# Attention with an adapter: one stacked fp32r product for the adapter's values, three orders moved, the causal mask in bf16

## The chip, the cores and the metric

The kernel runs on one core of a Trainium2 chip. The metric is the device time of one execution in microseconds; the time before is 2753.98 us, the median of three runs. Shorter is better.

## The reference, cut to what matters

One block of a transformer: adaLN, attention with an adapter, projection, then a mixture of experts. T = 2048 tokens, C = 1024, 32 heads of 32 columns, 10 adapter rows. The part that the change touches is this:

```python
scores = jnp.einsum('bhqd,bhkd->bhqk', q, k) / jnp.sqrt(jnp.asarray(hd, x.dtype))
scores = jnp.where(causal, scores, jnp.asarray(-jnp.inf, x.dtype))
attn = jax.nn.softmax(scores, axis=-1)
y = jnp.einsum('bhqk,bhkd->bhqd', attn, v)
...
ascores = jnp.einsum('bhqd,xhkd->bhqk', q, ak) / jnp.sqrt(jnp.asarray(C, x.dtype))
ascores = gating[0] * jax.nn.softmax(ascores.astype(jnp.float32), axis=-1).astype(q.dtype)
y = y + jnp.einsum('bhqk,xhkd->bhqd', ascores, av)
```

Everything else (the layernorms, q, k, v, the projection and the experts) is the same before and after.

## The kernel before, in words

Three stages follow one another: `front` (layernorm, modulation, q, k and v, the adapter's probabilities `a_prob` and values `av`), `attention`, and `tail` (projection, router, experts). The diff is in `attention`.

Attention takes four heads at a time (HG = 4, a group; there are G = 8). A unit is one group with one chunk of 512 queries (`qc` of 0 to 3); an iteration `i` of the outer loop has two groups, so W = 8 units and 80 steps. A step is one block of 128 keys of a unit, for four heads: for each head `score` makes the scores product (L1112, with a mask product L1116 on the diagonal), and then `look` works off what `order` lists for this slot. Behind the four slots come `multiply` (probabilities times values of two steps before, into `y_acc`, L1132), and in odd steps `add_up` (the softmax sums, into `total`, L1145).

`order` is a list written out ahead of the loop. Its entries are `see` (a scores product with queries and keys exchanged, L1065, from which VectorE takes the row maxima of a later group, L1278 or, masked, L1284), `turn` (the maxima are transposed), `ask` (the adapter's probabilities of a unit are transposed, L1078) and `give` (the adapter's values times these, L1084). `share` deals the entries of a step to its four slots: the first three get one each, the last gets the rest. Every entry writes one of the three banks of `seen`, in turn; TensorE waits before entry n until VectorE has freed entry n - 3. VectorE frees a bank itself: after a `see` with the reduce, after ask with `keep_turned` (a copy to `a_turn`, L1324), after give with `divide` (y_own times the inverse of the sums, L1332, then the adapter's part added, L1335; the bank is freed at L1314). ask stands in step last+6 of its unit's last step, give in step last+8, both in the second slot of an odd step.

ScalarE makes the exponentials (L1248) and takes `y_acc` and `total` out. GpSimd adds the probabilities of two steps for `add_up` (`two`, L1391, in two halves of two heads) and splits y into a high and a low part (L1397, L1399). SP issues the loads: q and k of the next group (L935), v (L1027), a broadcast of the inverses (L979), the stores of y (L985), `a_prob` for the next ask (L994, step last+3) and `a_v` for the next group (L998, behind the store in step last+9 of every fourth unit). In the last iteration `w_proj` is split too, partly by VectorE (L1356).

Ahead of the loop stands the head: 76 `see` products with their reduces, while SP loads the first group and the constants, and GpSimd scales the adapter's values with `gating` (L1368) and sets rows and buffers (L1371, L1373, L1374).

## Time and profile before

| | |
|---|---|
| median of three runs | 2753.98 us (2748.05 to 2754.27) |
| the profiled execution, its own time | 2743.23 us |
| its span | 2741.4 us |
| TensorE busy | 2517.3 us, 92% |
| VectorE busy | 1617.9 us, 59% |
| GpSimd busy | 1280.5 us, 47% |
| ScalarE busy | 1021.2 us, 37% |

PE is TensorE, PEld its weight loads, DVE is VectorE, ACT is ScalarE, POOL is GpSimd, SPq is SP's queue; a row with q after the engine is the engine's sequencer. A row of the timeline has the start in us from the start of the span, the time it took, the engine, the line, what it wrote and read, how many instructions were merged, and in brackets how long the engine had been idle and what ended that. A row of a group has busy time and mean time in ns, then the idle time before. A row of the stretches has the stretch, its length, the busy time of PE, PEld, DVE, ACT and POOL (with the number of instructions), the granted clock of TensorE as a share of full speed, the DMA engines' share and GB/s.

### The profile page before, as it was taken

To read this page: it belongs to the slowest core of one execution; us is meant where nothing else is said; L and a number is where in the kernel's file an instruction comes from. 1 tells how busy PE (TensorE), PEld (TensorE's weight loads), DVE (VectorE), ACT (ScalarE), POOL (GpSimd) and SP (SyncE) were. 2 spreads that over 40 slices of the span, in tenths; PEclk is the share of its full clock that TensorE was granted. 3 is DMA by queue.
4 is the path that set the end of the run, shared out by engine and by line. 5 is a ranking of instruction groups with operands and counts; after the bars stand their busy time and mean duration, and the time that the engine had idled before them with its cause. 6 is when DMAs were issued, how large, how long until landed. Compare 5 with 4: busy or idle time off the path is not lost. (4 is left out here: it accounts for less than half of the span.)

```text
span 2741.4 us, 39398 instructions
## 1 busy us (share of the span) xinstructions
PE 2517.3 (92%) x13399; PEld 1620.9 (59%) x13399; DVE 1617.9 (59%) x3227; ACT 1021.2 (37%) x1829; POOL 1280.5 (47%) x823
## 2 busy tenths in 40 slices
PE   6799999999599999999999999998979975999997
PEld 4667777777444444444444444444368764888885
DVE  5545565410277666767666766778236654767776
ACT  3421111110035555555555555555601111444443
POOL 4452342200436666666666666665723443333332
PEclk9999999999679999999999999999989987999998
DMA  7356555321624141413233141512356754878885
...
DMA packets 223212, 369.10 MB, mean 135 GB/s; under 512 B 43614, under 2 KB 103070, under 8 KB 222926
## 3 DMA queue, kind: packets, MB, share of 16 engines
...
q14 instruction: 67, 0.55, 0.1%
...
## 5 line engine op out<-in xcount | busy, mean ns | idle before, releaser
L1248 ACT ACTIVATE t_prob<-t_scores_psum 128x512 f32<-128x512 f32 (+3 forms) x1280 | 611.6, 537 | 528.7 <-PE t_scores_psum L1116 286.3
L1391 POOL TENSOR_TENSOR t_two<-t_prob 128x1024 f32<-128x1024 f32 (+1 forms) x321 | 687.1, 2161 | 242.7 <-ACT t_prob L1248 138.8
L1065 PE MATMUL t_seen_psum<-t_k_stack,t_q_stack 96*128 96x512 f32 (+3 forms) x1283 | 524.7, 421 | 60.5 <-DMA t_k_stack<-scratch_k_lo 22.6
L1278 DVE TENSOR_REDUCE t_part<-t_seen_psum 128x1 f32<-128x512 f32 x768 | 482.1, 683 | 158.4 <-PE t_seen_psum L1065 149.5
L1112 PE MATMUL t_scores_psum<-t_q_stack,t_k_stack 97*128 97x512 f32 (+3 forms) x1280 | 505.6, 406 | 5.5 <-ACT t_prob L1248 4.3
L1112 PEld LDWEIGHTS t_scores_psum<-t_q_stack,t_k_stack 97*128 97x128 f32 x1280 | 242.1, 190 | 332.0 <-ACT t_prob L1248 179.3
L1284 DVE CUSTOM_DVE_ANT_0 t_seen_psum<-t_seen_psum,t_causal 128x128 f32<-128x128 f32 (+3 forms) x515 | 248.9, 507 | 140.2 <-PE t_seen_psum L1065 128.0
L1065 PEld LDWEIGHTS t_seen_psum<-t_k_stack,t_q_stack 96*128 96x128 f32 x1283 | 257.2, 201 | 121.8 <-DVEq L1314 36.2
L1132 PE MATMUL t_y_acc_psum<-t_prob,t_v 128*32 128x512 f32 (+3 forms) x2560 | 312.8, 562 | 0.0
L1672 PE MATMUL acc_psum<-z_e_hi,z_x_hi 128*128 128x512 f32 x576 | 227.9, 396 | 0.0
L1674 PE MATMUL acc_psum<-z_e_hi,z_x_lo 128*128 128x512 f32 x576 | 224.9, 390 | 0.0
L1673 PE MATMUL acc_psum<-z_e_lo,z_x_hi 128*128 128x512 f32 x576 | 224.4, 390 | 0.0
L696 PE MATMUL f_acc_psum<-hT_hi,f_w_hi 128*128 128x512 f32 x512 | 209.6, 409 | 1.7 <-POOL f_w_lo L538 1.2
L697 PE MATMUL f_acc_psum<-hT_lo,f_w_hi 128*128 128x512 f32 x512 | 202.2, 395 | 0.0
L698 PE MATMUL f_acc_psum<-hT_hi,f_w_lo 128*128 128x512 f32 x512 | 201.9, 394 | 0.0
L550 POOL TENSOR_TENSOR f_y<-f_y,f_y_hi 128x512 fp32r<-128x512 f32 x64 | 82.7, 1292 | 234.0 <-PE f_turned_psum L680 153.3
L1145 PE MATMUL t_total_psum<-t_two,t_ones 128*32 128x512 f32 (+1 forms) x1296 | 167.3, 590 | 1.9 <-POOL t_two L1391 1.9
L288 ACT ACTIVATE f_y_hi<-f_y 128x512 fp32r<-128x512 f32 x64 | 40.4, 631 | 253.2 <-DVEq L447 253.0
L1674 PEld LDWEIGHTS acc_psum<-z_e_hi,z_x_lo 128*128 128x128 f32 x576 | 108.3, 188 | 22.9
L1742 ACT ACTIVATE z_x_hi<-z_turned_psum 128x1024 fp32r<-128x1024 f32 x38 | 38.7, 1018 | 222.9 <-PE z_turned_psum L1658 222.9
L1673 PEld LDWEIGHTS acc_psum<-z_e_lo,z_x_hi 128*128 128x128 f32 x576 | 108.5, 188 | 21.5
L1672 PEld LDWEIGHTS acc_psum<-z_e_hi,z_x_hi 128*128 128x128 f32 x576 | 108.4, 188 | 21.4
...
## 6 DMA issues: line engine op xcount, KB each, us to landing
...
t_q_stack<-scratch_q_hi SPq DMA_DIRECT2D x64, 256.0 KB, 5.5
t_k_stack<-scratch_k_hi SPq DMA_DIRECT2D x64, 256.0 KB, 4.9
...
scratch_y_hi<-t_y_own SPq DMA_DIRECT2D x33, 256.0 KB, 2.6
```

The lines of the kernel that those rows point to most:

```text
L696: nc.tensor.matmul(acc[:, n % 2], lhs[0], rhs[0], start=(k == 0), stop=False)
L697: nc.tensor.matmul(acc[:, n % 2], lhs[0], rhs[1], start=False, stop=False)
L1065: nc.tensor.matmul(seen[:, n % BANKS, 0:width], q_stack[par][0:STACK, h, t0:t0 + P], k_stack[par][0:STACK, h, c * CH:c * CH + width], star ...
L1112: last = nc.tensor.matmul(scores[:, score_bank(step, h), c0:CH], k_stack[par][0:TOPS, h, kt * P:(kt + 1) * P], q_stack[par][0:TOPS, h, qc ...
L1132: last = nc.tensor.matmul(y_acc[h * D:(h + 1) * D, c0:CH], v[par][:, kt, h * D:(h + 1) * D], prob[:, step % RING, h, c0:CH], start=(kt == ...
L1248: nc.scalar.activation(prob[:, step % RING, h, c0:CH], scores[:, score_bank(step, h), c0:CH], ACT.Exp, scale=1.0 / math.sqrt(D)).then_inc( ...
L1278: nc.vector.tensor_reduce(dst, seen[:, n % BANKS], AX.X, ALU.max).then_inc(seen_free, 1)
L1284: nc.vector.tensor_tensor_reduce(out=at, in0=at, in1=causal[:, CH - width:CH], scale=1.0, scalar=MASKED, op0=ALU.add, op1=ALU.max, accum_o ...
L1391: nc.gpsimd.tensor_tensor(two[:, pair % 2, heads, c0:CH], a, b, ALU.add).then_inc(two_ready, 1)
L1672: nc.tensor.matmul(acc[:, s, col], x_hi[:, s, k], e_hi[:, k, col], start=(k == 0), stop=False)
L1673: nc.tensor.matmul(acc[:, s, col], x_hi[:, s, k], e_lo[:, k, col], start=False, stop=False)
L1674: last = nc.tensor.matmul(acc[:, s, col], x_lo[:, s, k], e_hi[:, k, col], start=False, stop=(k == KC - 1))
```

## The change

give becomes one fp32r product over 120 rows. `a_v` is stacked in memory from the high part (twice) and the low part of the 40 rows, arranged so that the part of `a_turn` that is made by subtraction lies in rows 64 to 103; `a_turn` is the transposed probabilities three times, of which one is reduced to its low part. For that `a_prob` is loaded three times side by side (three DMAs of 160-byte pieces), ask transposes 120 columns, and `keep_turned` has a copy of 120 rows and then a subtract of 40. The stacked values are made at the start, by GpSimd and ScalarE, and written by five DMAs in place of one.

The three orders: SP loads the first q and k ahead of `v_own` and `gating`; ask and give are inserted one entry earlier, which puts them at the end of the last slot of the even step before; `divide` multiplies y_own with the inverse before it waits for give. The causal mask is kept in bf16, VectorE's masked reduce reads it so, and the mask product takes its last 128 columns in place of `after_b`; the constant `after` is no longer loaded.

```diff
@@ -785,6 +785,7 @@
     ROW = HG * 16
     TOPS = STACK + 1
     AK = HG * A
+    LOW = slice(D * 2, D * 2 + AK)
     with ExitStack() as ctx:
         sb = lambda name, shape, dt=F32: ctx.enter_context(nc.sbuf_tensor(f"t_{name}", shape, dt))
         pb = lambda name, shape: ctx.enter_context(nc.psum_tensor(f"t_{name}_psum", shape, F32))
@@ -795,28 +796,29 @@
             q_stack[b], k_stack[b] = sb(f"q_stack{b}", [P, HG, T], F32R), sb(f"k_stack{b}", [P, HG, T], F32R)
         v = [sb(f"v{b}", [P, NT, P]) for b in (1, 0)][::-1]
         p_raw = [v[0][:, c * KC:(c + 1) * KC, :].rearrange("p a n -> p (a n)") for c in range(2)]
-        ident, gating = sb("ident", [P, P]), sb("gating", [P, 1])
-        a_prob, a_v = sb("a_prob", [P, TPC, AK]), sb("a_v", [AK, P])
-        causal = sb("causal", [P, CH])
-        ident_b, after_b = sb("ident_b", [P, P], BF16), sb("after_b", [P, P], BF16)
+        ident = sb("ident", [P, P])
+        a_prob, a_v = sb("a_prob", [P, TPC, 3, AK]), sb("a_v", [3 * AK, P], F32R)
+        causal = sb("causal", [P, CH], BF16)
+        ident_b = sb("ident_b", [P, P], BF16)
         ones = sb("ones", [P, D])
         part = sb("part", [P, HG * TPC, NQ])
         top = sb("top", [P, HG * TPC])
         minus_top = sb("minus_top", [HG * TPC, 2, P], F32R)
         prob, two = sb("prob", [P, RING, HG, CH]), sb("two", [P, 2, HG, CH])
-        y_own, both = sb("y_own", [P, 2, CH]), sb("both", [P, 2, CH])
+        with ExitStack() as inner:
+            a_turn = inner.enter_context(nc.sbuf_tensor("t_a_turn", [3 * AK, CH], F32R))
+        both, y_own = sb("both", [P, 2, CH]), sb("y_own", [P, 2, CH])
         whole, inverse = both[:, 0], both[:, 1]
-        a_turn = both[0:AK, 0]
-        v_own = both[0:AK].rearrange("p b n -> p (b n)").rearrange("p (g n) -> p g n", n=P)
+        v_own, v_top = (at[0:AK].rearrange("p b n -> p (b n)").rearrange("p (g n) -> p g n", n=P) for at in (both, y_own))
         tall = sb("tall", [P, 2, CH // D])
         y = sb("y", [P, CH])
-        after = y_own[:, 0, 0:P]
+        gating, causal_f = tall[:, 0, 0:1], y[:, :]
         seen = pb("seen", [P, BANKS, CH])
         scores = pb("scores", [P, BANKS, CH])
         y_acc, total = pb("y_acc", [P, CH]), pb("total", [P, CH])
 
-        v_own_loaded, v_gated, v_kept = sm("v_own_loaded"), sm("v_gated"), sm("v_kept")
-        a_v_loaded, a_prob_loaded, a_turn_ready = sm("a_v_loaded"), sm("a_prob_loaded"), sm("a_turn_ready")
+        v_own_loaded, v_gated, v_top_done, v_low_done, v_stacked = sm("v_own_loaded"), sm("v_gated"), sm("v_top_done"), sm("v_low_done"), sm("v_stacked")
+        a_v_loaded, a_prob_loaded, a_top_done, a_turn_ready = sm("a_v_loaded"), sm("a_prob_loaded"), sm("a_top_done"), sm("a_turn_ready")
         consts_loaded, ones_set = sm("consts_loaded"), sm("ones_set")
         one_rows_set = sm("one_rows_set")
         first_loaded = [sm(f"first_loaded{c}") for c in range(NQ + 1)]
@@ -889,7 +891,7 @@
         given = sorted(((last_step(wi) + lag) % STEPS, lag, what, wi - W * (last_step(wi) + lag >= STEPS))
                        for wi in range(W) for lag, what in ((ASK_LAG, "ask"), (GIVE_LAG, "give")))
         for step, _, what, wi in given[::-1]:
-            order.insert(until(AHEAD + PACE * step) + 1, (what, 0, wi, 0, 0, 0))
+            order.insert(until(AHEAD + PACE * step), (what, 0, wi, 0, 0, 0))
         entries_of = lambda step: range(until(AHEAD + PACE * step), until(AHEAD + PACE * (step + 1)))
         assert STEPS % RING == 0
         END = until(AHEAD + PACE * STEPS)
@@ -943,21 +945,24 @@
 
         @block.sync
         def _(sp):
-            for h in range(HG):
-                sp.dma_start(v_own[h * A:(h + 1) * A], av[h * D:h * D + A, :, :]).then_inc(v_own_loaded, 16)
-            sp.dma_start(gating[:, :], consts["gating"].rearrange("(a n) -> a n", a=1).broadcast_to([P, 1])).then_inc(v_own_loaded, 16)
             for c in range(NQ):
 
                 for part in range(len(PARTS)):
                     load_part(sp, 0, ds(0), slice(c * CH, (c + 1) * CH), part, first_loaded[c])
                 if c == 0:
-                    for dst, name in ((ident[:, :], "ident"), (causal[:, :], "causal"), (after, "after")):
+                    for dst, name in ((ident[:, :], "ident"), (causal_f, "causal")):
                         sp.dma_start(dst, consts[name]).then_inc(consts_loaded, 16)
-                if c == 1:
-                    sp.wait_ge(v_gated, 1)
-                    sp.dma_start(a_v_d.rearrange("g r n -> r g n"), v_own).then_inc(v_kept, 16)
+                    for h in range(HG):
+                        sp.dma_start(v_own[h * A:(h + 1) * A], av[h * D:h * D + A, :, :]).then_inc(v_own_loaded, 16)
+                    sp.dma_start(gating, consts["gating"].rearrange("(a n) -> a n", a=1).broadcast_to([P, 1])).then_inc(v_own_loaded, 16)
             sp.dma_start(v[0][:, :, :], v_d[0]).then_inc(first_loaded[NQ], 16)
-            sp.wait_ge(v_kept, 16)
+            sp.wait_ge(v_top_done, 1)
+            sp.wait_ge(v_low_done, 1)
+            at = LOW.start - AK
+            for rows, src in (((0, AK), v_top), ((AK, LOW.start), v_own[0:at]), ((LOW.start, 2 * AK), v_top[at:AK]),
+                              ((2 * AK, LOW.stop), v_top[0:at]), ((LOW.stop, 3 * AK), v_own[at:AK])):
+                sp.dma_start(a_v_d[:, slice(*rows), :].rearrange("g r n -> r g n"), src).then_inc(v_stacked, 16)
+            sp.wait_ge(v_stacked, 16 * 5)
             for entry in order[:HEAD]:
                 if entry[0] == "turn":
                     sp.wait_ge(minus_ready, unit_of(entry) + 1)
@@ -991,11 +996,12 @@
                 if n < 0:
                     return
                 sp.wait_ge(a_turn_ready, n + 1)
-                sp.dma_start(a_prob[:, :, :].rearrange("p j k -> p (j k)"),
-                             a_prob_d[group_of(i, wi), UNITS[wi][1]].rearrange("g p k -> (g p) k")).then_inc(a_prob_loaded, 16)
+                src = a_prob_d[group_of(i, wi), UNITS[wi][1]].rearrange("g p (j k) -> (g p) j k", k=AK)
+                for x in range(3):
+                    sp.dma_start(a_prob[:, :, x], src).then_inc(a_prob_loaded, 16)
 
             def load_v(g):
-                sp.dma_start(a_v[:, :], a_v_d[g]).then_inc(a_v_loaded, 16)
+                sp.dma_start(a_v[:, :].bitcast(F32), a_v_d[g]).then_inc(a_v_loaded, 16)
 
             def finish(i, step):
 
@@ -1066,22 +1072,22 @@
                                  k_stack[par][0:STACK, h, c * CH:c * CH + width], start=True, stop=True).then_inc(seen_ready, 1)
 
             def turn_top(base, real, n, w):
-                pe.wait_ge(consts_loaded, 48)
+                pe.wait_ge(consts_loaded, 32)
                 pe.wait_ge(top_ready, w + 1)
                 pe.wait_ge(seen_free, base + real[n - 2] + BANKS)
                 nc.tensor.transpose(seen[0:HG * TPC, n % BANKS, 0:P], top[:, :], ident[:, :]).then_inc(seen_ready, 1)
 
             def ask(n, into):
 
-                pe.wait_ge(a_prob_loaded, 16 * (n + 1))
+                pe.wait_ge(a_prob_loaded, 48 * (n + 1))
                 for j in range(TPC):
-                    last = nc.tensor.transpose(into[0:AK, j * P:(j + 1) * P], a_prob[:, j], ident[:, :])
+                    last = nc.tensor.transpose(into[0:3 * AK, j * P:(j + 1) * P], a_prob[:, j].rearrange("p x k -> p (x k)"), ident[:, :])
                 last.then_inc(seen_ready, 1)
 
             def give(n, into):
                 pe.wait_ge(a_turn_ready, n + 2)
                 pe.wait_ge(a_v_loaded, 16 * (n // NQ + 1))
-                nc.tensor.matmul(into, a_v[:, :], a_turn, start=True, stop=True).then_inc(seen_ready, 1)
+                nc.tensor.matmul(into, a_v[:, :], a_turn[:, :], start=True, stop=True).then_inc(seen_ready, 1)
 
             def hold(into):
 
@@ -1113,7 +1119,7 @@
                                         q_stack[par][0:TOPS, h, qc * CH + c0:(qc + 1) * CH], start=True, stop=(r < 0))
                 if r >= 0:
 
-                    last = nc.tensor.matmul(scores[:, score_bank(step, h), c0:c0 + P], ident_b[:, :], after_b[:, :],
+                    last = nc.tensor.matmul(scores[:, score_bank(step, h), c0:c0 + P], causal[:, CH - P:CH], ident_b[:, :],
                                             start=False, stop=True)
                 last.then_inc(scores_ready, 1)
 
@@ -1217,7 +1223,10 @@
         def _(act):
             nc.scalar.preload_act_table(ACT.Exp)
             act.sem_inc(exp_done, BANKS)
-            act.wait_ge(v_kept, 16)
+            act.wait_ge(v_gated, 1)
+            act.wait_ge(ones_set, 3)
+            nc.scalar.activation(v_top.bitcast(F32R), v_own, ACT.Copy).then_inc(v_top_done, 1)
+            act.wait_ge(v_stacked, 16 * 5)
             act.wait_ge(sums_set, 2)
 
             def take_y(i, wi):
@@ -1267,9 +1276,10 @@
                 dve.sem_inc(row_loaded[b], ROW)
             nc.vector.memset(ones[:, :], 1.0).then_inc(ones_set, 1)
 
-            dve.wait_ge(consts_loaded, 48)
+            dve.wait_ge(consts_loaded, 32)
             nc.vector.tensor_copy(ident_b[:, :], ident[:, :]).then_inc(ones_set, 1)
-            nc.vector.tensor_copy(after_b[:, :], after).then_inc(ones_set, 1)
+            nc.vector.tensor_copy(causal[:, :], causal_f).then_inc(ones_set, 1)
+            dve.wait_ge(ones_set, 3)
 
             def largest(base, real, n, qc, c, h, j):
                 dve.wait_ge(seen_ready, base + real[n] + 1)
@@ -1309,8 +1319,7 @@
                 elif what == "turn":
                     negate(i * ITEMS, real_of[i], n, i * W + w, i * (W // 2) + w // 2, w % 2)
                 elif what in ("ask", "give"):
-                    dve.wait_ge(seen_ready, i * ITEMS + real_of[i][n] + 1)
-                    (keep_turned if what == "ask" else divide)(i, qc, seen[:, n % BANKS])
+                    (keep_turned if what == "ask" else divide)(i, qc, seen[:, n % BANKS], i * ITEMS + real_of[i][n])
                     dve.sem_inc(seen_free, 1)
 
             def invert(i, wi):
@@ -1318,13 +1327,16 @@
                 dve.wait_ge(tall_loaded, (i * W + wi + 3) * 16)
                 nc.vector.reciprocal(tall[:, 1], tall[:, 0]).then_inc(inverted, 1)
 
-            def keep_turned(i, wi, at):
+            def keep_turned(i, wi, at, before):
 
                 n = i * W + wi
-                nc.vector.tensor_copy(a_turn, at[0:AK]).then_inc(a_turn_ready, 1)
+                dve.wait_ge(seen_ready, before + 1)
+                nc.vector.tensor_copy(a_turn[:, :], at[0:3 * AK]).then_inc(a_top_done, 1)
+                dve.wait_ge(a_top_done, n + 2)
+                nc.vector.tensor_tensor(a_turn[LOW], at[LOW], a_turn[LOW].bitcast(F32), ALU.subtract).then_inc(a_turn_ready, 1)
                 dve.wait_ge(a_turn_ready, n + 2)
 
-            def divide(i, wi, at):
+            def divide(i, wi, at, before):
                 n = i * W + wi
                 dve.wait_ge(inverse_loaded, (n + 2) * (16 * HG))
                 dve.wait_ge(y_free, n + 2)
@@ -1332,6 +1344,7 @@
                 nc.vector.tensor_tensor(own, own, inverse, ALU.mult).then_inc(norm_step, 1)
                 dve.wait_ge(norm_step, n + 2)
                 dve.wait_ge(stored, (n + 3) * 32)
+                dve.wait_ge(seen_ready, before + 1)
                 nc.vector.tensor_tensor(y[:, :], at, own, ALU.add).then_inc(y_ready, 1)
                 dve.wait_ge(y_ready, n + 3)
 
@@ -1357,16 +1370,17 @@
             for step in range(INV_LAG + 1):
                 finish(G // 2, step)
             for x, (keep, at) in enumerate(((keep_turned, y_acc), (divide, total))):
-                dve.wait_ge(seen_ready, (G // 2 - 1) * ITEMS + real_of[-1][END] + x + 1)
-                keep(G // 2, -1, at[:, :])
+                keep(G // 2, -1, at[:, :], (G // 2 - 1) * ITEMS + real_of[-1][END] + x)
 
         @block.gpsimd
         def _(pool):
             pool.sem_inc(y_lo_done, 1)
             pool.sem_inc(two_ready, 3)
             pool.wait_ge(v_own_loaded, 80)
-            nc.gpsimd.tensor_scalar(v_own, v_own, gating[0:AK, 0:1], None, ALU.mult).then_inc(v_gated, 1)
-            pool.wait_ge(v_gated, 1)
+            nc.gpsimd.tensor_scalar(v_own, v_own, gating[0:AK], None, ALU.mult).then_inc(v_gated, 1)
+            pool.wait_ge(v_top_done, 1)
+            nc.gpsimd.tensor_tensor(v_own.bitcast(F32R), v_own, v_top, ALU.subtract).then_inc(v_low_done, 1)
+            pool.wait_ge(v_low_done, 1)
             for b in range(2):
                 nc.gpsimd.memset(k_stack[b][STACK:TOPS, :, :].bitcast(F32), 1.0).then_inc(one_rows_set, 1)
                 pool.wait_ge(one_rows_set, b + 1)
@@ -2049,7 +2063,7 @@
             p_parts = [inner.enter_context(nc.sbuf_tensor(n, [P, KC, C], F32R)) for n in ("p_hi", "p_lo")]
             acc = inner.enter_context(nc.psum_tensor("acc_psum", [P, MT, C], F32))
         with semaphores(nc) as sem:
-            attention(nc, sem, consts, a_prob_d, av, scratch("a_v", [G, HG * A, P]), (q_hi, q_lo), (k_hi, k_lo), v, (y_hi, y_lo), scratch("inverse", [HG, CH]), w_proj, p_parts, acc)
+            attention(nc, sem, consts, a_prob_d, av, scratch("a_v", [G, 3 * HG * A, P]), (q_hi, q_lo), (k_hi, k_lo), v, (y_hi, y_lo), scratch("inverse", [HG, CH]), w_proj, p_parts, acc)
         with semaphores(nc) as sem:
             tail(nc, sem, consts, mod_rows, p_parts, acc, expert_w, (y_hi, y_lo), x, h2, table, out)
```

## Rows read from the trace of the kernel before

**Rows 1.** The page: the span, and busy time of the engines.

```profile
span 2741.4 us, 39398 instructions
...
PE 2517.3 (92%) x13399; PEld 1620.9 (59%) x13399; DVE 1617.9 (59%) x3227; ACT 1021.2 (37%) x1829; POOL 1280.5 (47%) x823
```

**Rows 2.** Stretches: the attention loop, and around a fall of the clock.

```profile
778.70:1990.00 1211.30, 1165.76 (x7099) 542.49 (x7098) 816.61 (x1896) 651.48 (x1362) 779.90 (x448) 0.97 0.31 72
1192.50:1199.30 6.80, 6.19 (x30) 2.94 (x26) 4.10 (x13) 4.24 (x8) 5.04 (x3) 1.00 0.34 88
1199.30:1202.80 3.50, 3.50 (x17) 0.59 (x16) 1.45 (x6) 0.00 (x0) 1.54 (x2) 0.51 0.30 109
```

**Rows 3.** Groups by shape, 782 to 1990 us.

```profile
L1084 PE MATMUL t_seen_psum<-t_both,t_a_v 40*128 40x512 f32 x62 | 36.1, 664 | 4.4 <-DMA t_a_v<-scratch_a_v 4.4
...
L1332 DVE TENSOR_TENSOR t_y_own<-t_y_own,t_both 128x512 f32<-128x512 f32 x32 | 24.2, 756 | 29.2 <-PE t_seen_psum L1084 29.2
```

**Rows 4.** L1314, the freeing of a bank: who waited (us, times).

```profile
  PE t_seen_psum L1065: 18.3, 31
```

**Rows 5.** Timeline around the give at 1196 us, three engines.

```profile
1192.76 4.70 POOL L1391 TENSOR_TENSOR t_two<-t_prob 128x1024 f32<-128x1024 f32 x2 [2.09 <-PE t_total_psum L1145]
...
1194.71 0.70 DVE L1284 CUSTOM_DVE_ANT_0 t_seen_psum<-t_seen_psum,t_causal 128x512 f32<-128x512 f32 x1
...
1196.22 1.12 PE L1084 MATMUL t_seen_psum<-t_both,t_a_v 40*128 40x512 f32 x2
...
1197.38 0.69 DVE L1332 TENSOR_TENSOR t_y_own<-t_y_own,t_both 128x512 f32<-128x512 f32 x1 [0.82 <-PE t_seen_psum L1084]
...
1198.10 0.69 DVE L1335 TENSOR_TENSOR t_y<-t_seen_psum,t_y_own 128x512 f32<-128x512 f32 x1
...
1198.91 0.50 PE L1065 MATMUL t_seen_psum<-t_k_stack,t_q_stack 96*128 96x512 f32 x1 [0.61 <-DVEq L1314]
```

**Rows 6.** Timeline at two places where VectorE and GpSimd meet.

```profile
969.26 2.49 DVE L1278 TENSOR_REDUCE t_part<-t_seen_psum 128x1 f32<-128x512 f32 x4 [1.15 <-PE t_seen_psum L1065]
...
969.33 4.68 POOL L1391 TENSOR_TENSOR t_two<-t_prob 128x1024 f32<-128x1024 f32 x2
...
973.77 0.79 DVE L1332 TENSOR_TENSOR t_y_own<-t_y_own,t_both 128x512 f32<-128x512 f32 x1 [0.77 <-PE t_seen_psum L1084]
...
975.39 0.50 PE L1065 MATMUL t_seen_psum<-t_k_stack,t_q_stack 96*128 96x512 f32 x1 [0.62 <-DVEq L1314]
...
1876.47 4.69 POOL L1391 TENSOR_TENSOR t_two<-t_prob 128x1024 f32<-128x1024 f32 x2
...
1878.81 2.90 DVE L1356 TENSOR_TENSOR p_lo<-t_v,p_hi 128x512 fp32r<-128x512 f32 x1
...
1882.37 0.80 PE L1065 MATMUL t_seen_psum<-t_k_stack,t_q_stack 96*128 96x512 f32 x1 [1.00 <-DVE t_part L1278]
```

**Rows 7.** Timeline: one load of a_v and the give that waited.

```profile
1419.89 0.40 SPq L998 DMA_DIRECT2D t_a_v<-scratch_a_v  x1
...
1424.25 1.70 PE L1084 MATMUL t_seen_psum<-t_both,t_a_v 40*128 40x512 f32 x2 [1.41 <-DMA t_a_v<-scratch_a_v]
```

**Rows 8.** Timeline: one load of a_prob and its ask.

```profile
955.61 0.44 SPq L994 DMA_DIRECT2D t_a_prob<-scratch_a_prob  x1
...
964.75 0.60 PE L1078 MATMUL t_seen_psum<-t_ident,t_a_prob 128*40 128x128 f32 x4
```

**Rows 9.** DMA issues by line: size, us to landing.

```profile
t_v<-scratch_v SPq DMA_DIRECT2D x28, 256.0 KB, 3.8
```

**Rows 10.** Timeline at the start of the stage.

```profile
711.26 3.20 SPq L947 DMA_DIRECT2D t_both<-av  x4
...
715.03 0.43 SPq L935 DMA_DIRECT2D t_q_stack<-scratch_q_hi  x1
...
720.34 13.90 POOL L1371 MEMSET t_k_stack<- 1x8192 f32 x2
...
732.29 2.04 DVE L1271 CAST t_ident_b<-t_ident 128x128 bf16<-128x128 f32 x1 [20.21 <-DMA t_y_own<-in_after]
```

## The prediction

> **What bounds the kernel now.** I read the page first: TensorE is busy for 92% of a span of 2741.4 us [rows 1]. The busy times cut by stretch then show that the attention stage runs from 778.7 to 1990 us with TensorE at 96% and its granted clock at 0.97 [rows 2]. Every change of this diff inside the loops falls in that stretch, so a microsecond is worth something only where TensorE stands still or streams. The groups by shape give the rows that the change touches: the adapter's product L1084, recorded as two matmuls for each fp32 product, 62 rows for 31 products in the loop, and the product y_own*inverse L1332, one for each of 32 units there [rows 3]. Who waits for the line that frees a bank after ask or give (L1314) is the next view: matmuls of L1065 stood still 31 times for it, 18.3 us in all [rows 4]. The order of one such place is in the timeline [rows 5]: give runs from 1196.22 to 1197.34; VectorE multiplies from 1197.38 to 1198.07 and adds until 1198.79; only then does the fourth `see` of the step start, at 1198.91, after 0.61 us of idle. Right behind it the clock falls: over 1199.30 to 1202.80 the granted clock is 0.51, the lower of its two levels (1.2 GHz of 2.4), where it was 1.00 in the 6.8 us before [rows 2]. A mean clock of 0.97 over 1211.3 us is 1211.3 x 0.03 = 36 us of lost time in the stage. So a give costs three things: the fp32 product, the wait for VectorE, and often a drop of the clock.
>
> **The product.** Give becomes one fp32r matmul of 120 rows. A 512-column fp32r product is recorded with 0.50 us, tail and all (L1065 at 1198.91), the fp32 give with 1.12 [rows 5]. So at least 0.6 us of TensorE work goes per give, and I take 0.7. Ask transposes 120 columns in place of 40, in the same four matmuls, and their weight loads overlap other matmuls; I take nothing, and as a bound 0.2 us per ask, 6 us.
>
> **The moved wait, which decides.** Give moves from the second slot of an odd step to the end of the even step before, and divide now does y_own*inverse ahead of its wait for give. VectorE reaches that multiply as soon as it has reduced the fourth `see` product of the even step. In [rows 5] that is 1194.71 + 0.70 for the reduce, about 1195.4. GpSimd is then in its pair of adds `two`, 1192.76 to 1197.46, 2.35 us each, so the second has begun at 1195.1. What a VectorE op with two SBUF tensors does in that position is shown by L1356 and by one late multiply [rows 6]: L1356 started at 1878.81, was recorded for 2.90 us and ended at 1881.71, 0.55 us after GpSimd's 1881.16; L1332 started at 973.77, GpSimd ended at 974.01 and it ended at 974.56, again 0.55 us later. Free of that, L1332 takes 0.69 us [rows 5]. Before the change the multiply came after give and started at GpSimd's very end; now it is held for most of an add. New chain at the same place: GpSimd ends 1197.46, multiply ends 1198.01, add (0.69) ends 1198.72, bank free 1198.75. TensorE meanwhile has done give, the value products and two scores and sees, and needs that bank for the third `see` of the odd step near 1197.0. It waits some 1.8 us; the fourth then waits for VectorE's first reduce and starts near 1199.2, against 1198.91 now: 0.3 us later, although 0.7 us of product is gone. That stands for the 16 units with qc 1 and 2. For the 8 with qc 3, whose odd step has only 512-column `see`s, the reduce is longer, and I take 0.45 us. In the 8 with qc 0, of which 973.77 is one, the add would end at 974.56 + 0.69 = 975.25, one reduce more gives 975.95, against 975.39 [rows 6]. There the gives that wait for DMA today (next part) gain back as much, so I take 0.2 for that kind. The sum is 16 x 0.3 + 8 x 0.45 + 8 x 0.2 = 10 us later. The lower bound is a multiply that isn't held: below, as a rival. The upper bound is 32 x 0.7 = 22 us.
>
> The Trainium skill, "SBUF — State Buffer", section on the two separate sides of SBUF, says the port pair that VectorE and GpSimd share is an exclusive lock for a whole instruction, and that a VectorE op with two SBUF inputs contends with a GpSimd op that reads SBUF. The trace agrees, with 2.90 us beside 0.69. Read strictly, the op would take its full 0.69 behind the release instead of 0.55, so by the page the sum would be 32 x 0.14 = 4 us more.
>
> **The adapter values arrive later than their use.** a_v is loaded in every fourth unit behind the broadcast of the next unit's inverse, a chain that starts from TensorE's last total and isn't shortened. The load issued at 1419.89 held give until 1424.25, 1.41 us of idle [rows 7]. So it lands up to 4.4 us after issue; other issues come up to 4.1 us ahead of a give that needn't wait. Give now comes about 2 us of TensorE time earlier (one value product and two or three others), so seven of eight wait some 1.5 to 3.4 us, 16 us in all by my estimate, where today the waits of 1.4 us are the exception. This is no term of its own: in those units the held multiply and add end no sooner anyhow, and it is already in the 0.2.
>
> **The probabilities in three loads.** SP issues three in place of one, each of 512 pieces of 160 bytes. Today 9.1 us pass from issue to ask, 955.61 to 964.75 [rows 8]; ask moves 1.9 us forward, leaving 7.2. An equal number of pieces, of 512 bytes, is in each v load, which lands in 3.8 us [rows 9]. Two further issues of 0.44 give 4.7 us: hidden, at nothing. If the three went one after another, 11.4 us, ask would wait up to 4.2 us. Keep_turned on VectorE gets a second op of 0.7 us with one PSUM input. It is hidden, since the value products (1.0 us) now lie between ask and the bank's next use; without that cover it would cost 32 x 0.7 = 22 us. The causal mask in bf16 and the slice of it as mask weights keep shapes and types of the products: nothing.
>
> **The clock.** It fell behind stretches in which give and a wait of 0.6 us met, or a wait of 1.4 us stood alone. The fp32 give goes, but the wait becomes 1.8 us, plus a short one, in 24 units and 1.5 to 3 us in seven. In the trace a multiply held by GpSimd did just this: VectorE came back at 1881.71 and TensorE stood still until 1882.37 [rows 6]. I take a third more low clock than now less what falls on idle: 8 us later, bounds -15 (the falls halve) and +20.
>
> **Start and end.** The four v_own loads and gating move behind the first q and k loads, which are issued from 711.26 in place of 715.03; `after` is no longer loaded; and VectorE's first cast, recorded for 2.04 us from 732.29 because GpSimd's memset ran until 734.24, now comes while GpSimd still waits for v_own [rows 10]. The sees of the head, bound by VectorE, start some 5 us sooner. GpSimd's chain starts some 10 us later and has one op of 3 us more, and a wait for ScalarE; it stays hidden, since the products that need its memsets start only at 778.7. Without that cover the 5 us would be lost, and 0 is the bound. The last give saves 1 us.
>
> Sum: 10 + 8 - 5 - 1 = 12 us. The profiled execution reported 2743.2 us (2741.4 span and 1.8 around it), which becomes 2755; the median of the runs is 10.8 above it, so I forecast 2754 + 12 = 2766 us.
>
> **Rivals.** (1) The multiply isn't held, because VectorE gets there before GpSimd's second add, or GpSimd shifts. The margin is 0.3 us in the place worked out, and 0.1 at 971.7, where the reduces end at 971.75 and GpSimd's second add began at 971.67 [rows 6]. Then the bank is free at 1195.4 + 0.69 + 0.72 = 1196.8, just when needed: the old wait (18.3 / 31 = 0.6) and the product go, 24 x 1.3 = 31 us and 3 in the others; low clock remains only behind the a_v waits, 18 us less; with 6 from start and end it is 58 us faster, 2696. It decides from a multiply of 0.69 us instead of 2.4. For it: GpSimd's pace depends on its own waits. Against: both places have VectorE behind the boundary, and the pace of both engines there follows the same total on TensorE. 0.14 for all units, 0.05 for some of them (2725 to 2745).
> (2) As forecast, but the falls of the clock stay as many as now: 4 us, 2758, no change that can be told. 0.31.
> (3) The three loads of probabilities land after ask: 24 short-slack units by up to 4.2 us, and more low clock, some 2830. Against: [rows 9]. 0.05. The Trainium skill, "DMA: Bandwidth & Descriptors", Specifications, has pieces under 512 bytes fall to read-modify-write; no row shows its price, and by the page this rival would be likelier.
>
> **How the numbers follow.** The held multiply has 0.76 with (2) and the forecast (0.45) in it. A measurement of this kernel tells 0.3%, 8 us. Slower: 0.45 and most of (3), 0.48. Same: 0.31. Faster: 0.21. The range leaves out the whole of (1) and most of (3): 2716 to 2786.
>
> **What would show it.** L1332's successor with a median near 2.4 us instead of 0.69 and `see` waiting 1.5 us or more behind give shows the held multiply; 0.69 refutes it and makes the forecast wrong by 50 us or more. Idle of give on DMA near 16 us shows the a_v part; idle of ask on DMA refutes the probabilities' part. The stage's clock at 0.96 shows the clock term, 0.98 or more refutes it. VectorE's first reduce near 729.5 shows the start.

## The result, and the profile after

The changed kernel takes 2788.8 us (median of 4 runs, 2780.2 to 2795.7) against 2751.0 us for the kernel before on the same chip: a ratio of 1.0145, 95% interval 1.011 to 1.0179. It is slower, as forecast, but by about 38 us instead of 12, and 2.8 us above the range. (The ratios are the measured ones, each with its own interval; they can differ from the quotient of the two medians, here 1.0137, by some tenths of a per cent.)

The page of the changed kernel gives its span and busy times, beside [rows 1]:

```profile
span 2793.9 us, 39437 instructions
...
PE 2537.0 (91%) x13367; PEld 1642.4 (59%) x13367; DVE 1676.0 (60%) x3260; ACT 1026.1 (37%) x1830; POOL 1292.9 (46%) x824
```

This profiled execution is the slowest of the changed kernel's runs, and that of before was 8 us under its median, so the spans lie 52.5 us apart where the medians lie 38. The 52.5 divide into four parts: the front's end, 6.3 us later in this execution (717.53 in place of 711.26 for the stage's first load); the start of the stage, 6.9 us shorter; the attention loop, 50.3 us longer; and what follows, 2.8 us longer.

The loop is best read between its own ends, from the first product into y_acc to the last score product. The busy times cut there, for the kernel before:

```profile
778.71:1983.95 1205.24, 1161.56 (x7047) 540.86 (x7046) 816.60 (x1896) 650.38 (x1359) 774.79 (x445) 0.97 0.31 73
```

and for the changed kernel:

```profile
778.05:2033.56 1255.51, 1176.18 (x7017) 557.68 (x7016) 878.57 (x1928) 654.10 (x1359) 776.38 (x445) 0.94 0.33 74
```

Length less TensorE's busy time is its idle time: 43.7 us before, 79.3 after, 35.7 more. Busy time grew by 14.6 us although give lost some 22 us of work (36.1 us in [rows 3], 13.6 us below). So some 37 us of busy time are the same matmuls at the lower clock. The clock's own records in the two traces agree: inside the loop it falls to its lower level 16 times before and 27 times after, and stays there for 69 us in all before and 155 after. The mean is 0.94 for 0.97.

Who waited for the line that frees a bank behind ask and give, now L1323, beside [rows 4]:

```profile
  PE t_seen_psum L1071: 51.8, 45
```

The groups by shape, 778.7 to 1990 us, beside [rows 3] (one matmul per give now; the multiply is L1344, keep_turned's two ops, a copy and a subtraction, are L1334 and L1336):

```profile
L1344 DVE TENSOR_TENSOR t_y_own<-t_y_own,t_both 128x512 f32<-128x512 f32 x31 | 73.1, 2360 | 0.5
...
L1336 DVE TENSOR_TENSOR t_a_turn<-t_seen_psum,t_a_turn 40x512 fp32r<-40x512 f32 x31 | 21.5, 695 | 1.1
...
L1334 DVE CAST t_a_turn<-t_seen_psum 120x512 fp32r<-120x512 f32 x31 | 21.2, 683 | 0.3
...
L1090 PE MATMUL t_seen_psum<-t_a_turn,t_a_v 120*128 120x512 f32 x30 | 13.6, 452 | 10.7 <-DMA t_a_v<-scratch_a_v 8.4 <-DVE t_part L1288 2.3
```

One give in the timeline, beside [rows 5]:

```profile
1219.49 4.71 POOL L1405 TENSOR_TENSOR t_two<-t_prob 128x1024 f32<-128x1024 f32 x2 [2.63 <-PE t_total_psum L1151]
...
1221.08 0.39 PE L1090 MATMUL t_seen_psum<-t_a_turn,t_a_v 120*128 120x512 f32 x1
1222.04 2.71 DVE L1344 TENSOR_TENSOR t_y_own<-t_y_own,t_both 128x512 f32<-128x512 f32 x1
1224.79 0.69 DVE L1348 TENSOR_TENSOR t_y<-t_seen_psum,t_y_own 128x512 f32<-128x512 f32 x1
...
1225.59 0.44 PE L1071 MATMUL t_seen_psum<-t_k_stack,t_q_stack 96*128 96x384 f32 x1 [2.00 <-DVEq L1323]
```

The multiply starts just after GpSimd's second add has begun (1221.85), and ends at 1224.75, 0.55 us behind GpSimd's 1224.20. TensorE stands still for 2.00 us. The clock behind it, by stretches:

```profile
1212.00:1225.60 13.60, 11.12 (x64) 5.30 (x63) 10.94 (x25) 7.84 (x16) 9.43 (x4) 1.00 0.31 78
1225.60:1229.00 3.40, 3.40 (x15) 1.11 (x19) 2.01 (x8) 0.60 (x1) 1.89 (x2) 0.60 0.16 58
```

And an ask, with VectorE's two ops:

```profile
1213.19 0.60 PE L1084 MATMUL t_seen_psum<-t_ident,t_a_prob 128*120 128x128 f32 x4
...
1213.49 0.25 DVE L1328 RECIPROCAL t_tall<-t_tall 128x16 f32<-128x16 f32 x1 [0.59 <-DMA t_tall<-t_both]
1213.66 1.22 DVE L1288 TENSOR_REDUCE t_part<-t_seen_psum 128x1 f32<-128x512 f32 x2
...
1214.80 0.68 DVE L1334 CAST t_a_turn<-t_seen_psum 120x512 fp32r<-120x512 f32 x1
...
1215.52 0.69 DVE L1336 TENSOR_TENSOR t_a_turn<-t_seen_psum,t_a_turn 40x512 fp32r<-40x512 f32 x1
...
1216.32 0.44 PE L1071 MATMUL t_seen_psum<-t_k_stack,t_q_stack 96*128 96x384 f32 x1 [0.40 <-DVEq L1323]
```

Ask's last transpose ends at 1213.79, but VectorE is still behind: it waited for `tall` and then has two reduces, so its copy starts a whole microsecond later. The subtraction ends at 1216.21, and TensorE has waited since 1215.92. Without the subtraction the bank would have been free at about 1215.5, by the end of the copy. The wider transposes cost nothing: one takes a mean of 272 ns here, 273 before.

### The profile page after: what moved, and what is told of

Same layout as the page of the kernel before. It is cut to its first block and busy times, and to the rows that moved or that the text cites. A ratio compares the mean times of both kernels' runs of the same rounds, so it can differ in the third digit from the quotient of the medians.

```text
span 2793.9 us, 39437 instructions
## 1 busy us (share of the span) xinstructions
PE 2537.0 (91%) x13367; PEld 1642.4 (59%) x13367; DVE 1676.0 (60%) x3260; ACT 1026.1 (37%) x1830; POOL 1292.9 (46%) x824
## 5 line engine op out<-in xcount | busy, mean ns | idle before, releaser
L1071 PE MATMUL t_seen_psum<-t_k_stack,t_q_stack 96*128 96x512 f32 (+3 forms) x1283 | 542.3, 434 | 84.2 <-DVEq L1323 51.8
L1118 PE MATMUL t_scores_psum<-t_q_stack,t_k_stack 97*128 97x512 f32 (+3 forms) x1280 | 512.1, 411 | 6.4 <-ACT t_prob L1257 5.0
L1118 PEld LDWEIGHTS t_scores_psum<-t_q_stack,t_k_stack 97*128 97x128 f32 x1280 | 249.0, 195 | 319.6 <-ACT t_prob L1257 159.0
L1071 PEld LDWEIGHTS t_seen_psum<-t_k_stack,t_q_stack 96*128 96x128 f32 x1283 | 265.2, 207 | 156.0 <-DVEq L1323 66.9
L1138 PE MATMUL t_y_acc_psum<-t_prob,t_v 128*32 128x512 f32 (+3 forms) x2560 | 320.1, 574 | 0.0
L1151 PE MATMUL t_total_psum<-t_two,t_ones 128*32 128x512 f32 (+1 forms) x1296 | 174.4, 613 | 1.9 <-POOL t_two L1405 1.9
L1913 DVE SCALAR_TENSOR_TENSOR z_x_in<-acc_psum,z_ids_a,z_gb 128x1024 f32<-128x1024 f32 x36 | 46.1, 1280 | 136.5 <-DMA z_ids_a<-scratch_table 136.5
```

Of the source, the lines that this page charges most:

```text
L1071: nc.tensor.matmul(seen[:, n % BANKS, 0:width], q_stack[par][0:STACK, h, t0:t0 + P], k_stack[par][0:STACK, h, c * CH:c * CH + width], star ...
L1118: last = nc.tensor.matmul(scores[:, score_bank(step, h), c0:CH], k_stack[par][0:TOPS, h, kt * P:(kt + 1) * P], q_stack[par][0:TOPS, h, qc ...
L1138: last = nc.tensor.matmul(y_acc[h * D:(h + 1) * D, c0:CH], v[par][:, kt, h * D:(h + 1) * D], prob[:, step % RING, h, c0:CH], start=(kt == ...
```

## The experiments

Fifteen kernels ran. The table holds for each the ratio of the times to the kernel before on the same chip, and from its profiled execution the loop as above (length, TensorE busy, idle) with the waits for the line that frees ask's and give's bank. A wait is put down to the ask or give that ran last before it, within 6 us; each entry has the us in all and the number of waits. "Give for a_v" is give's own wait for the load of the adapter values. The last column has how often the clock fell to its lower level inside the loop, and for how many us in all it was there.

| kernel | ratio | loop | busy | idle | behind give | behind ask | give for a_v | low clock |
|---|---|---|---|---|---|---|---|---|
| before | 1 | 1205.2 | 1161.6 | 43.7 | 16.8, 28 | 2.0, 9 | 4.4, 4 | 16, 69 |
| changed | 1.0145 | 1255.5 | 1176.2 | 79.3 | 38.0, 23 | 12.8, 21 | 8.4, 5 | 27, 155 |
| e1 divide back | 1.0148 | 1248.0 | 1166.1 | 81.9 | 38.2, 23 | 12.8, 21 | 11.3, 7 | 23, 129 |
| e2 places back | 1.0092 | 1248.0 | 1162.1 | 85.9 | 41.7, 30 | 23.3, 30 | none | 27, 135 |
| e3 both back | 1.0103 | 1230.6 | 1142.3 | 88.3 | 42.5, 30 | 23.4, 30 | none | 23, 91 |
| e4 before, moved | 1.0094 | 1233.0 | 1171.2 | 61.8 | 23.6, 24 | 2.0, 7 | 17.2, 8 | 18, 96 |
| e5 e3, no low part | 1.0020 | 1203.5 | 1134.1 | 69.4 | 43.9, 30 | 2.0, 9 | 1.4, 2 | 21, 74 |
| e6 before, two ops | 1.0145 | 1236.3 | 1173.2 | 63.1 | 19.6, 30 | 22.3, 30 | none | 21, 93 |
| e7 e3, multiply on GpSimd | 0.9873 | 1162.6 | 1114.4 | 48.2 | 2.5, 11 | 23.3, 30 | none | 6, 30 |
| e8 e7, parts on GpSimd | 0.9741 | 1135.5 | 1105.5 | 30.0 | 0.3, 2 | 2.0, 9 | 3.3, 5 | 3, 13 |
| e9 e8, new orders | 0.9748 | 1150.8 | 1114.8 | 36.1 | none | 2.2, 7 | 6.9, 4 | 9, 37 |
| e10 before, multiply on GpSimd | 0.9832 | 1161.4 | 1135.4 | 26.0 | 0.2, 1 | 1.8, 8 | 4.1, 4 | 4, 25 |
| e11 changed, parts on GpSimd | 1.0064 | 1239.0 | 1161.9 | 77.1 | 43.0, 26 | 2.0, 7 | 14.1, 7 | 31, 125 |
| e12 changed, multiply on GpSimd | 0.9828 | 1173.2 | 1129.1 | 44.1 | none | 12.5, 21 | 11.1, 7 | 11, 64 |
| e13 e8, add done twice | 0.9804 | 1156.4 | 1107.2 | 49.3 | 22.5, 30 | 2.0, 9 | 3.4, 4 | 4, 16 |
| e14 three times | 0.9969 | 1209.4 | 1136.1 | 73.3 | 43.4, 30 | 2.0, 9 | 4.7, 6 | 16, 85 |
| e15 four times | 1.0148 | 1252.9 | 1160.9 | 92.0 | 66.8, 30 | 1.9, 8 | none | 31, 139 |

### Which of the orders costs

**e1**, divide waits for give first again; **e2**, the old places; **e3**, both; **e4**, the new places alone, in the kernel before:

```diff
 # e1, e3
                 n = i * W + wi
+                dve.wait_ge(seen_ready, before + 1)
                 dve.wait_ge(inverse_loaded, (n + 2) * (16 * HG))
...
-                dve.wait_ge(seen_ready, before + 1)
                 nc.vector.tensor_tensor(y[:, :], at, own, ALU.add).then_inc(y_ready, 1)
 # e2, e3; e4 is the opposite edit
-            order.insert(until(AHEAD + PACE * step), (what, 0, wi, 0, 0, 0))
+            order.insert(until(AHEAD + PACE * step) + 1, (what, 0, wi, 0, 0, 0))
```

> The changed kernel (2788.8 us) with divide's order put back: y_own*inverse waits for give again. Theory A, place and GpSimd: with give at the end of the even step the multiply is held by GpSimd's second add whichever side of give it starts on, and ends 0.55 us behind that add; the order of divide alone is then worth little: 2781 to 2797. Theory A', the order of divide itself is the loss: the wait for the multiply goes back to 0.6 us, 2735 to 2750. Rival B, the second VectorE op behind ask and the wider ask cost the time: no change, 2781 to 2797, and the same holds for e3.

> The changed kernel with ask and give back in their old places in the order (second slot of the odd step), divide's new order kept. Theory A: the multiply starts late in GpSimd's second add and ends where it did before, so the waits are those of before, the product's 0.7 us x 31 is saved and 5 us at the start: 2751 - 22 - 5 = 2724, range 2712 to 2736; median of the multiply between 0.9 and 2 us. Theory A': a multiply held by GpSimd still costs, 2765 to 2789. Rival B: 2770 to 2797, the gain of the places is small.

> The changed kernel with both the places of ask and give and divide's order back: what is left is the 120-row product, the three loads of probabilities, the mask and the order of the start. Theory A: 2724, range 2712 to 2736, multiply with a median near 0.70 us, stage clock 0.97 or more. Rival B (keep_turned's second op, three loads): 2765 or more, with the waits of the places behind ask as in the changed kernel.

> The kernel before with only the places of ask and give moved, by the same edit of one line; the fp32 product, the single load, keep_turned's one op and divide's order stay. Theory A: the multiply starts behind give, inside GpSimd's second add, and is held to its end; the waits and the low clock of the changed kernel come back, and the longer product (0.7 us x 31) stands on top in part: 2785 to 2812. Rival B: places cost little, 2745 to 2760.

Measured: e1 1.0148 (1.012 to 1.0176), e2 1.0092 (1.0058 to 1.0126), e3 1.0103 (1.0075 to 1.0131), e4 1.0094 (1.0059 to 1.0128). Divide's order is worth nothing that can be told, at either place. The places cost some 12 to 15 us in the changed kernel (e1 less e3, the changed kernel less e2); each of these ratios has an interval of 8 to 10 us either way, so the size is loose. Alone they cost 26 us (less than theory A and more than B expected of e4), 13 of these as waits for a_v. Theory A fell at e2 and e3, for which it had 2736 at most: with both orders back the kernel is still 28 us slower than before. B had that time right, but the waits behind ask are larger than in the changed kernel, not as there. The trace of e3 shows two reasons. Waits behind ask went from 2.0 to 23.4 us. And the multiply is held at the old place too; here is one, in the timeline of e3 (the multiply is L1345 there):

```profile
1206.15 2.39 POOL L1405 TENSOR_TENSOR t_two<-t_prob 128x1024 f32<-128x1024 f32 x1
1207.62 1.46 DVE L1345 TENSOR_TENSOR t_y_own<-t_y_own,t_both 128x512 f32<-128x512 f32 x1
1209.12 0.69 DVE L1348 TENSOR_TENSOR t_y<-t_seen_psum,t_y_own 128x512 f32<-128x512 f32 x1
...
1209.92 0.51 PE L1071 MATMUL t_seen_psum<-t_k_stack,t_q_stack 96*128 96x512 f32 x1 [1.49 <-DVEq L1323]
```

GpSimd ends at 1208.54 and the multiply 0.54 us later. The shorter product lets VectorE reach the multiply some 0.7 us sooner, inside GpSimd's add, and the multiply lasts about as much longer: its median is 1.46 us, and the waits behind give grew from 16.8 to 42.5 us, more than the 22 us that the product gave.

### The second op behind ask

**e5** is e3 without the subtraction, so it leaves out the low part and doesn't compute what the reference asks; **e6** is the kernel before with the copy done twice:

```diff
 # e5
-                nc.vector.tensor_copy(a_turn[:, :], at[0:3 * AK]).then_inc(a_top_done, 1)
-                dve.wait_ge(a_top_done, n + 2)
-                nc.vector.tensor_tensor(a_turn[LOW], at[LOW], a_turn[LOW].bitcast(F32), ALU.subtract).then_inc(a_turn_ready, 1)
+                nc.vector.tensor_copy(a_turn[:, :], at[0:3 * AK]).then_inc(a_turn_ready, 1)
 # e6
-                nc.vector.tensor_copy(a_turn, at[0:AK]).then_inc(a_turn_ready, 1)
+                nc.vector.tensor_copy(a_turn, at[0:AK]).then_inc(a_top_done, 1)
+                dve.wait_ge(a_top_done, n + 2)
+                nc.vector.tensor_copy(a_turn, at[0:AK]).then_inc(a_turn_ready, 1)
```

> e3 (2777.2 us: the 120-row product, the places and divide's order as before) without keep_turned's second op: the subtraction that makes the low part of the turned probabilities is left out, and those rows keep the high part. Theory T1: that op is late for the see product two banks on, 0.8 us at each of 30 asks, 23 us of TensorE's waits against 2 before, and the clock falls behind some of them; without it 2745 to 2758. Rival T2, the cost of e3 lies in its other parts (three loads of probabilities, the start, the tiles' places): 2768 or more.

> The kernel before (2751.8 us) with one thing added: keep_turned copies twice, the second op waiting for the first. Theory T1: the waits for VectorE behind ask go from 2.0 us to 20 to 25 us, and the kernel takes 2768 to 2785. Rival T2: 2745 to 2760, the second op is hidden.

Measured: e5 2746.4 us, 1.002 (1.0001 to 1.0039); e6 2776.4 us, 1.0145 (1.012 to 1.0171). Both are as T1 has it. One more op of 0.68 us on VectorE behind ask, and nothing else, makes the kernel before about as slow as the changed one: 40 us by the ratio, 33 by the medians of that chip. The waits of e6:

```profile
PE t_seen_psum L1065 <- DVEq L1314: 36.4, 54, 1.2
```

### The multiply and the split, off VectorE

**e7** and **e8** build on e3; **e9** gives e8 the changed kernel's places and order of divide; **e10** moves the multiply alone in the kernel before; **e11** and **e12** move the split alone and the multiply alone in the changed kernel:

```diff
 # the multiply (e7 to e10, e12)
-                nc.vector.tensor_tensor(own, own, inverse, ALU.mult).then_inc(norm_step, 1)
...
+            def normalise(i, wi):
+                n = i * W + wi
+                pool.wait_ge(inverse_loaded, (n + 2) * (16 * HG))
+                pool.wait_ge(y_free, n + 2)
+                own = y_own[:, wi % 2]
+                nc.gpsimd.tensor_tensor(own, own, inverse, ALU.mult).then_inc(norm_step, 1)
...
+                for wi in ended(i, step, SPLIT_LAG - 2):
+                    normalise(i, wi)
 # the split (e8, e9, e11); one load of a_prob, one copy in keep_turned, a_v stacked as high, low, high
+            def halve(i, wi):
...
+                pool.wait_ge(a_prob_loaded, 16 * (n + 1))
+                raw = a_prob[:, :, 2]
+                for x in range(2):
+                    nc.gpsimd.tensor_copy(a_prob[:, :, x].bitcast(F32R), raw).then_inc(a_prob_top, 1)
+                pool.wait_ge(a_prob_top, 2 * (n + 1))
+                nc.gpsimd.tensor_tensor(raw, raw, a_prob[:, :, 0], ALU.subtract).then_inc(a_prob_low, 1)
...
+                for wi in ended(i, step, PROB_LAG + 1):
+                    halve(i, wi)
```

> e3 with y_own*inverse taken off VectorE: GpSimd does it two steps sooner, where it stands idle between its pairs of adds; VectorE only adds the give. Theory T1: in e3 the multiply lasts 1.46 us in the median in place of 0.69, because the shorter product lets VectorE reach it while GpSimd still adds, and the product's gain is lost there (waits behind give 42.5 us against 16.8 before); with the multiply gone these waits fall below 10 us and the kernel takes 2732 to 2748. Rival T3: what VectorE does behind give isn't what sets TensorE's waits, or GpSimd's extra 1.3 us makes two and total late by as much: 2770 or more.

> e7, and the high and low parts of the probabilities are made on GpSimd before ask, on the 128x160 tile, from a single load; keep_turned is one copy again and the adapter's values are stacked in three stores. Theory T1: both waits gone, the product's gain kept: 2700 to 2725. Rival T3: GpSimd's work is what counts, 2745 or more.

> e8 (ratio 0.974 to the kernel before) with the changed kernel's places of ask and give and its order of divide. Theory P1, the places cost by themselves: give comes ahead of its adapter values (17.2 us of TensorE's waits in 8 gives in e4), so e8 plus 12 to 25 us, ratio 0.978 to 0.984, idle of give on DMA 15 us or more. Theory P2, the places cost only through VectorE's waits, which are gone: ratio 0.972 to 0.976, as e8.

> The kernel before with only y_own*inverse moved to GpSimd, two steps sooner. Theory T1: VectorE's chain behind give is shorter by one op of 0.7 us, so the 16.8 us of waits behind give go to a few; the fp32 product's 1.12 us stays on TensorE's path: 15 to 22 us faster, ratio 0.992 to 0.995. Rival: the multiply was not in the way in the kernel before, ratio 0.998 to 1.002.

> The changed kernel (ratio 1.0145 to the kernel before) with only the high and low parts of the probabilities made on GpSimd; the multiply stays on VectorE ahead of its wait for give. Theory T1: only the 12.8 us of waits behind ask and the low clock behind them go, 13 to 25 us: ratio 1.005 to 1.010; the multiply keeps a median above 2.3 us. Rival, the multiply's hold alone made the loss: 1.012 or more.

> The changed kernel with only y_own*inverse moved to GpSimd; keep_turned keeps its second op. Theory T1: the 38.0 us of waits behind give fall below 8 us and with them low clock, 40 to 60 us: ratio 0.993 to 1.000; waits behind ask stay near 13 us and those of give on its adapter values rise from 8.3 us to some 17. Rival, the hold only hides other waits: 1.006 or more.

Measured: e7 2707.9 us, 0.9873 (0.9838 to 0.9909); e8 2667.7 us, 0.9741 (0.9722 to 0.9759); e9 2686.5 us, 0.9748 (0.9717 to 0.9778); e10 2704.5 us, 0.9832 (0.9814 to 0.9851); e11 2769.9 us, 1.0064 (1.0047 to 1.0081); e12 2708.5 us, 0.9828 (0.98 to 0.9855). The directions are those of T1, and e11 is in its range. e7, e8, e10 and e12 gained more than was expected of them. e10 shows why: its loop is 43.9 us shorter, 17.7 of it idle, as expected, and 26.2 of it busy time of the same matmuls, which was not:

```profile
778.95:1940.30 1161.35, 1135.38 (x7047) 538.85 (x7047) 793.27 (x1864) 650.30 (x1359) 811.61 (x477) 0.99 0.32 76
```

So the kernel before already paid 46 us for a multiply of 0.69 us: 17 in waits and most of the rest in low clock, with 4 falls in e10 where there were 16. On GpSimd it costs 1.28 us, where that engine waited for the inverse anyhow (group by shape, e8):

```profile
L1404 POOL TENSOR_TENSOR t_y_own<-t_y_own,t_both 128x512 f32<-128x512 f32 x33 | 42.3, 1280 | 105.3 <-DMA t_both<-scratch_inverse 103.7 <-ACT t_prob L1254 1.6
```

e8, which computes all that the reference asks, is faster than both kernels, by 2.6% and by about 4%. Its loop:

```profile
771.66:1907.20 1135.54, 1105.53 (x7016) 536.64 (x7015) 793.36 (x1864) 647.59 (x1359) 844.52 (x570) 0.99 0.32 78
```

e9 is in P2's range: by the ratios the new orders can't be told from the old ones once VectorE is out of the way, and give waited for a_v for 6.9 us, not 15. But a cost of some 10 us isn't excluded: the medians, each against its own chip's, would put e9 10 us above e8, and its profiled loop is 15 us longer, with 9 falls of the clock in place of 3.

### What a wait costs in clock

**e13**, **e14** and **e15** repeat e8's add behind give once, twice and three times more (e14 shown as the loop that writes it):

```diff
+                for x in range(2):
+                    nc.vector.tensor_tensor(y[:, :], at, own, ALU.add).then_inc(again, 1)
+                    dve.wait_ge(again, 2 * (n + 1) + x + 1)
                 nc.vector.tensor_tensor(y[:, :], at, own, ALU.add).then_inc(y_ready, 1)
```

> e8 (attention loop 1135.5 us, TensorE idle in it 30.0 and busy 1105.5; ratio 0.974) with VectorE's add behind give done twice, so that the bank comes free 0.7 us later at 32 places. TensorE's idle grows by what of it isn't covered: 5 to 22 us. Theory C1, the low clock goes with the idle time, some 1.3 us of longer busy time per us of idle (as from e12 to the changed kernel, 47 over 35): busy +7 to +29, ratio 0.978 to 0.993. Theory C2, each wait draws the same low clock whatever its length: busy +35 to +45 here already, and hardly more in e14 and e15. Theory C3, short waits cost no clock (as the prediction's small term has it): busy +0 to +6.

> e8 with the add behind give done three times: the bank free 1.4 us later at 32 places. Idle 22 us above e13. C1: busy another 29 us above e13, ratio about 1.005. C2: busy within 8 us of e13, ratio about 0.997. C3: busy 10 to 45 us above e13.

> e8 with the add behind give done four times: 2.1 us later. Idle 22 us above e14. C1: busy another 29 us above e14, ratio about 1.024. C2: busy within 8 us of e13 and e14, ratio about 1.005. C3: the steepest step between e14 and e15 or e13 and e14, 40 us or more.

Measured: e13 0.9804 (0.9774 to 0.9834), e14 0.9969 (0.9951 to 0.9988), e15 1.0148 (1.0126 to 1.017). The loops of e13, e14 and e15, each from its own trace:

```profile
779.59:1936.03 1156.44, 1107.16 (x7017) 535.38 (x7016) 812.83 (x1896) 647.77 (x1359) 845.59 (x570) 0.99 0.33 76
```

```profile
770.86:1980.26 1209.40, 1136.14 (x7016) 543.58 (x7016) 835.63 (x1928) 648.72 (x1359) 845.12 (x570) 0.96 0.31 73
```

```profile
770.41:2023.31 1252.90, 1160.94 (x7017) 550.87 (x7016) 858.37 (x1960) 652.11 (x1359) 847.26 (x570) 0.94 0.30 70
```

Thirty waits of 0.75 us lengthened the busy time by 1.6 us, thirty of 1.45 us by 31, thirty of 2.2 us by 55. Theory C2 fell. C3 is right for the first step and C1 for the size of the two behind it (29 and 25 us of busy time, 29 expected), though its ratios were 0.008 to 0.009 too high. The medians bear the first step out: e13 is 19.9 us above e8, and its loop has 19.3 us more idle time. The falls show how the cost comes about: 3 in e8, 4 in e13, 16 in e14, 31 in e15. A wait does not draw a bit of low clock each time; some waits are followed by a fall and others are not. One wait of each kind shows it, by stretches; e13, where TensorE waited 0.73 us until 1181.58:

```profile
1172.00:1181.60 9.60, 8.79 (x53) 4.42 (x51) 6.74 (x22) 6.20 (x12) 6.74 (x4) 1.00 0.36 89
1181.60:1185.00 3.40, 3.40 (x23) 1.49 (x23) 2.01 (x8) 0.51 (x2) 3.32 (x4) 1.00 0.00 0
```

and e14, where it waited 1.46 us until 1189.40:

```profile
1179.00:1189.40 10.40, 8.87 (x52) 4.47 (x51) 7.55 (x23) 6.20 (x12) 6.88 (x4) 1.00 0.32 86
1189.40:1192.80 3.40, 3.40 (x17) 0.78 (x17) 1.66 (x6) 0.00 (x0) 3.15 (x3) 0.60 0.00 0
```

## Why the prediction was right and wrong

The runs form a path from the kernel before to the changed one, in us of 2751 by the ratios: the multiply taken off VectorE (e10), -46; the product with its split on GpSimd, the start and the mask (e8), -25; the new orders (e9), +2; the multiply back on VectorE (e11), +87; the split back on it, with the three loads (the changed kernel), +22. That is +40. Each ratio is known to 5 to 10 us either way, and another order of the steps could share the sum out otherwise; the split's 22 comes out the same from e9 to e12, with the multiply off VectorE. The start is 8 of the 25, read below. The forecast had +18 for product, waits, a_v and clock together; these are -46 - 25 + 8 + 2 + 87 = +26. It had 0 for keep_turned's second op; that is +22. It had -5 for the start, measured -7 in the changed kernel's own trace and -8 as the mean.

**The step that failed is "Keep_turned on VectorE gets a second op of 0.7 us ... It is hidden, since the value products (1.0 us) now lie between ask and the bank's next use".** It costs 22 us here (e11), of a miss of some 28 by the ratios, and 33 to 40 us alone in the kernel before (e6). The cover was counted from ask's end on TensorE. VectorE takes the turned probabilities only after the reduces that it still owes, 1.0 us later in the timeline above, and by then the value products are spent. The cover was there only in part: 21 waits of 12.8 us in all at the new places, 30 of 23.3 at the old ones (e2). And most of the price isn't idle time. From e11 to the changed kernel the waits behind ask grow by 10.8 us, but those behind give and for a_v shrink by 10.7; idle time grows by 2.2 us, busy time by 14.3, at the lower clock. So it is luck that the prediction's bound for a missing cover, 22 us, is the value measured: the bound counted 32 waits of 0.7 us and no clock. In e6 the idle time is 19 us more and the busy time 12.

**The clock, 8 us later, was mis-sized.** It is some 37 us in the profiled execution, beyond the prediction's bound of 20, of which the split accounts for 14 (busy 1176.2 to 1161.9 in e11); the two failures overlap by that much. The mean clock of the loop is 0.94, where the prediction's sign had 0.96. Time at the lower level more than doubled, where "a third more low clock than now" was taken from no row that priced a fall by the length of the wait. e13 to e15 price it, and the forecast wait of 1.8 us lies where each costs more than a microsecond of clock.

**The held multiply was right**, place, mechanism and size: a median of 2704 ns in place of 693, 32 of 33 multiplies ending 0.55 us behind a GpSimd add (27 of them 1.4 us long or more, the other five, of 0.95 to 0.97, caught by the last of the add), and 23 waits of 1.65 us on average, against 24 of 1.8. Rival 1 is refuted. The idle less the product is +13 us in the loop against +10 forecast, and +11 in e11, where the split is off VectorE; so the term of 10 was right. What the prediction did not see is that the order of divide hardly matters (e1): the multiply is held because give is earlier (e4, a median of 2.40 us with the old product) and, at the old place, because it is shorter (e3). The Trainium skill, "SBUF — State Buffer", section on the two separate sides of SBUF, has the shared port pair locked for a whole instruction by whichever of the two starts first; the trace agrees for a GpSimd add that began first, 2.71 us beside 0.69, except that the held multiply ended 0.55 us behind the add and not a full 0.69.

**The product** is worth its 22 us only where VectorE isn't the next wait: nothing in e5 (1.002), some 17 us from e10 to e8 (25 less 8 for the start).

**The adapter values.** Five gives waited 8.4 us in the changed kernel, not seven for 16; where VectorE delays TensorE less, the forecast number comes back: 17.2 us in 8 (e4), 14.1 in 7 (e11), 11.1 in 7 (e12). It was kept out of the sum, rightly.

**The three loads** were hidden: ask never waited for DMA, and each load landed in a median of 2.5 us, in the DMA issues by line. The one load of before, of the same 80 KB in pieces of 640 bytes, took 2.3. That refutes rival 3, the price for small pieces included; the two rows, changed kernel and before:

```profile
t_a_prob<-scratch_a_prob SPq DMA_DIRECT2D x96, 80.0 KB, 2.5
```

```profile
t_a_prob<-scratch_a_prob SPq DMA_DIRECT2D x32, 80.0 KB, 2.3
```

**Rival 2**, as many falls of the clock as now, is refuted by their count, 27 for 16. **The mask** was not tried alone; the masked 512-column reduce takes a mean of 716 ns (719 before) and the mask product 234 (232), so nothing shows a cost. **The chances** have two slips: the 0.05 of rival 1 at 2725 to 2745 lies inside the range and not outside it, and "faster" is 0.19 by the rivals listed, not 0.21.

**The start** was right in its cause and rather low in size. From the stage's first load to the first product into y_acc it takes 67.2 to 67.5 us in the four kernels with the old order (before, e4, e6, e10) and 58.7 to 60.5 in ten with the new one (the changed kernel, 717.53 to 778.05, and all up to e12 but those three). VectorE's first cast takes 0.23 us, not 2.04. The first reduce came at 732.3, not at 729.5, because the front ended 6.3 us later in this execution; counted from the stage's first load it came after 14.7 us in place of 23.1, so 8.3 us sooner where the prediction had some 5. **The end's** 1 us is below what the traces can tell.

Open: the changed kernel has 71 us more busy time than e8 for the same matmuls, with 59 us of waits behind give, behind ask and for a_v, 49 in all; e15 has 55 us more, with 67 us behind give, 30 waits. e3 to e1 points the same way: fewer idle microseconds at the new places, but 24 more of busy time. The clock falls no more often for it (27 times against 31, and 23 against 23), but it stays low longer in all: 155 us against 139, and 129 against 91. What keeps it low longer at the new places was not settled. Profiled executions of kernels with equal times, as e2 and e3, differ by 20 us in busy time, so part of this is scatter.
